# A fused retention and feed-forward block: the order of the first loads and the length of the warming

## The reference

```python
q1, k1 = apply_rotary(x @ Wq, x @ Wk)              # 4 heads of 64
v = x @ Wv                                         # 4 heads of 128
o = chunk_retention(q, k, v, gamma)                # decay gamma^distance, causal
o = rmsnorm(o, gn_weight) * silu(x @ Wg)
x = layernorm(x + o @ Wo)
h = silu(x @ (w_gate/127).T) * (x @ (w_up/127).T)  # hidden 768, integer weights
x = layernorm(x + h @ (w_down/127).T)
```

## Time and profile before

| | us |
|---|---|
| median of 3 runs | 427.47 |
| lowest and highest | 426.11, 428.21 |
| the profiled execution, its own time | 425.66 |
| its span, first to last instruction | 423.9 |

### The profile page before, as it was taken

How to read it: one execution, slowest core, us unless ns; L and a number is a source line. 1 busy time by engine, 2 the same in 40 slices (tenths; PEclk the granted TensorE clock), 3 DMA queues, 4 the chain that set the end, 5 groups by cost and what they waited for, 6 DMA issues and landing times.

```text
span 423.9 us, 12406 instructions
## 1 busy us (share of the span) xinstructions
PE 418.1 (99%) x4311; PEld 396.8 (94%) x4311; DVE 312.1 (74%) x907; ACT 259.0 (61%) x796; POOL 188.1 (44%) x330
## 2 busy tenths in 40 slices
PE   8999999999999999999999999999999999999995
PEld 7899999999999999999999999999999999999995
DVE  4999677678676778766777666777766777667785
ACT  6568755577566566566566566565666565565552
POOL 2522343445544344444354444354534354444465
PEclk9999999999999999999999999999999999999999
DMA  8931010201111011110001111011110010100002
GB/s 275 376 120 52 0 53 1 65 2 39 39 40 39 2 40 39 39 37 17 27 31 37 37 37 37 0 37 37 37 37 12 1 40 15 39 14 2 15 27 65
DMA packets 14327, 19.66 MB, mean 46 GB/s; under 512 B 1488, under 2 KB 9808, under 8 KB 14288
## 3 DMA queue, kind: packets, MB, share of 16 engines
q1 hardware_dynamic: 14144, 19.08, 13.8%
q10 hardware_dynamic: 144, 0.07, 0.1%
HBM read 14.94 MB, written 4.19 MB: 45 GB/s over the span
## 4 chain that ended last, share of the span: by engine, by line
PE 97%; DVE 1%; issue 0%; POOL 0%; ACT 0%; POOLq 0%; ACTq 0%; DVEq 0%
PE b_rows L463 29%; PE b_ffn L463 20%; PE b_rows L481 13%; PE b_rows L477 8%; PE b_head L639 7%; PE b_head L609 4%; PE b_turn L673 3%; PE b_head L605 3%; PE b_ffn L628 3%; PE b_turn L491 2%; PE b_state L658 2%; PE b_state L745 1%; DVE wf_int L1367 1%; PE b_rows L524 0%; PE b_ffn L658 0%
## 5 line engine op out<-in xcount | busy, mean ns | idle before, releaser
L1710 POOL TENSOR_TENSOR h_lo<-wf_int,h_hi 128x256 fp32r<-128x256 f32 x96 | 70.9, 740 | 97.3 <-ACT h_hi L1005 97.0
L463 PE MATMUL b_ffn<-x1T_hi,wf_hi 128*128 128x256 f32 x384 | 92.6, 278 | 0.1
L463 PE MATMUL b_ffn<-x1T_lo,wf_hi 128*128 128x256 f32 x384 | 92.1, 277 | 0.0
L463 PEld LDWEIGHTS b_ffn<-x1T_hi,wf_hi 128*128 128x128 f32 x384 | 72.2, 188 | 0.7 <-DVE wf_int L1344 0.5
L463 PEld LDWEIGHTS b_ffn<-x1T_lo,wf_hi 128*128 128x128 f32 x384 | 72.2, 188 | 0.0
L980 ACT ACTIVATE sq<-b_head 128x128 f32<-128x128 f32 x124 | 34.4, 277 | 50.5 <-PE b_head L639 47.5
L1005 ACT CAST h_hi<-wf_int 128x256 fp32r<-128x256 f32 x96 | 38.8, 404 | 40.6 <-DVE wf_int L1344 39.9
L1728 POOL TENSOR_TENSOR ve<-mv,eps 128x1 f32<-128x1 f32 x63 | 13.7, 217 | 87.3 <-DVE mv L1455 71.0
L481 PE MATMUL b_rows<-wp_hi,xT_lo 128*128 128x256 f32 x198 | 50.0, 277 | 0.0
L1344 DVE TENSOR_TENSOR wf_int<-b_ffn,wf_int 128x256 f32<-128x256 f32 x96 | 40.4, 421 | 11.8 <-ACT wf_int L994 9.0
L1446 DVE TENSOR_TENSOR z<-b_rows,x_sb 128x256 f32<-128x256 f32 x32 | 13.6, 425 | 44.7 <-PE b_rows L463 44.7
(11 more groups left out here) (158 smaller groups left out, 1227.4 us busy)
## 6 DMA issues: line engine op xcount, KB each, us to landing
xT_raw<-in_xT SPq DMA_DIRECT2D x16, 256.0 KB, 2.7
x_sb<-in_x SPq DMA_DIRECT2D x16, 256.0 KB, 2.7
out<-wf_int SPq DMA_DIRECT2D x30, 128.0 KB, 1.7
wf_int<-in_w_ffn SPq DMA_DIRECT2D x6, 384.0 KB, 6.3
wf_int<-in_w_proj SPq DMA_DIRECT2D x6, 256.0 KB, 4.2
rope_sb<-in_rope SPq DMA_DIRECT2D x4, 256.0 KB, 5.7
rope_q<-in_rope_by_row SPq DMA_DIRECT2D x2, 512.0 KB, 8.8
wo_raw<-in_w_o SPq DMA_DIRECT2D x1, 512.0 KB, 6.8
```

The lines of the kernel that those rows point to most:

```text
L463: mm = pe.matmul(dst, a, b, start=(i == 0 and j == 0 and not begun), stop=(i == n - 1 and j == len(passes) - 1 and not more), skip_group_c ...
L1710: pool.tensor_tensor(h_lo[:, ring, hb], h_full[:, u], h_hi[:, ring, hb].bitcast(F32), ALU.subtract).then_inc(h_split[j], 1)
```

## The change

ScalarE issues the load of W(0,0) itself, as its first instruction. SP's first load is now the x of tile 0 alone (128 KB), followed by the five other weight parts, and the x of tile 1 comes behind them, in front of the rope tables. The array of pair 0 is laid out by tile on the host so that each half is one piece of 1 KB in a row; its target in SBUF is two pieces of 512 bytes per partition. ScalarE casts the six weight parts one after the other and tile 1's x behind them. The warming has six products instead of eight. The same bytes are loaded in all.

```diff
-WARM_UP = 8
+WARM_UP = 6
...
+        xT_first_in = sem("xT_first_in")
...
-            def load_w_proj(c):
-                for k in range(KD):
+            def load_w_proj(c, parts=range(KD)):
+                for k in parts:
                     sp.dma_start(wp_raw[:, c, k], w_proj[c, k]).then_inc(wp_in[KD * c + k], 16)
 
-            load_xT(0, 0)
-            load_w_proj(0)
+            def load_xT_of_pair_0(tile):
+                part = xT[0:P, tile * KD * P:(tile + 1) * KD * P].rearrange("p (k n) -> p k n", k=KD)
+                sp.dma_start(xT_raw[:, 0, :, tile * P:(tile + 1) * P], part).then_inc((xT_first_in, xT_in[0])[tile], 16)
+
+            load_xT_of_pair_0(0)
+            load_w_proj(0, (1,))
             load_w_proj(1)
             load_w_proj(2)
+            load_xT_of_pair_0(1)
             sp.dma_start(rope_sb[:, 0], rope[0]).then_inc(rope_in[0], 16)
...
             def split_xT(s, q, t):
 
                 ring, at = t // 2, (t % 2) * P
-                act.wait_ge(xT_in[ring], 16 * (q + 1))
+                if is_slot(s, 0):
+                    act.wait_ge(xT_first_in, 16)
+                else:
+                    act.wait_ge(xT_in[ring], 16 * (q + 1))
...
+            act.dma_start(wp_raw[:, 0, 0], w_proj[0, 0]).then_inc(wp_in[0], 16)
             act.wait_ge(filled, 1)
             act.activation(silu_first[:], half_neg[:, 0:1], ACT.Silu)
...
             split_xT(0, 0, 0)
-            split_w_proj(0, 0)
-            split_xT(1, 0, 1)
-            split_w_proj(0, 1)
-            for c in (1, 2):
+            for c in range(3):
                 for k in range(KD):
                     split_w_proj(c, k)
+            split_xT(1, 0, 1)
...
+    xT = laid(x.reshape(-1, 2 * P, KD, P).transpose(0, 3, 2, 1))
+    xT[0] = laid(xT[0].reshape(P, KD, 2, P).swapaxes(1, 2)).reshape(P, KD, 2 * P)
...
-        "in_xT": laid(x.reshape(-1, 2 * P, KD, P).transpose(0, 3, 2, 1)).reshape(-1, KD * 2 * P),
+        "in_xT": xT.reshape(-1, KD * 2 * P),
```

## The result

| | before | changed |
|---|---|---|
| median of 22 runs each, us | 426.25 | 427.26 |
| lowest, highest, us | 425.23, 428.21 | 426.21, 429.29 |
| the profiled execution, us (span) | 425.66 (423.9) | 429.29 (427.6) |

The ratio of the changed kernel to the one before is 1.0024, 95% interval 1.0013 to 1.0034: about 1 us slower. The median came out where it was forecast (427.3), but only because the 22 runs of before have a lower median, 426.25, than the three that the forecast started from; against them the change cost 1 us where it was to give 0.2. The profiled execution of the changed kernel is its slowest of the 22, which has to be kept in mind when reading its rows.

What follows compares the result with a forecast made beforehand. TensorE, 99% busy, bounds the kernel and carries start changes to the end; its 0.4 to 0.45 us gain shrinks to 0.2 at slot 0's turn, waiting for rotation. Profiled 425.66 becomes 425.46, median 427.47 becomes 427.3; range 425.7 to 428.8 us.

Steps and rivals of the forecast that it cites:

- rival C: ScalarE's start: the table load goes before the W(0,0) issue, slot 1's first nine end 0.25 us later; median 427.7, chance 0.12.
- rival A: Start of slot 1: tile 1's x comes last and holds slot 1, 0.2 us later than before; median 427.7, chance 0.09.
- at half the size it comes at 3.1 to 3.4, I take 3.3: First load on SP: tile 0's x, halved, lands at 3.3 us instead of 3.42; its cast ends at 3.7.
- I take 3.7: W(0,0) from ScalarE's queue lands at 3.7 us instead of 4.06; first product at 4.4, 0.45 earlier, bounds 0.1 and 0.7.
- the hole at 2.2 us: DMA at 2.2 to 2.4 us, 113 GB/s: a second issuing queue may fill it, worth 0 to 0.2 us.
- up at about 7.1 as before: Slot 0 on TensorE: clock rises at about 7.1 us as before, so slot 0 ends at 10.0 instead of 10.47.
- rival B: Slot 0 on TensorE: less warming and a hole delay the clock, 0.2 us per slow product, +1.8; median 429.3, chance 0.09.
- slot 0's first products follow closely, as before: Slot 0's start: the prediction's argument against a later clock rise, which had cost +1.8 us and chance 0.09.
- hardly moves: 9.69, less 0 to 0.2: Rope table 0's load on SP: same bytes ahead, lands 0 to 0.2 us before 9.69; rotation starts at 9.6.
- the 0.2 us of gain: Slot 0's turn: the rotation's earlier start gives 0.2 us, bounds 0.1 and 0.4; the rest of TensorE's gain is waited off.
- S: Start loads, theory after the result: ScalarE's queue shares the DMA engines, so tile 0's x lands late; no chance given.

Runs made afterwards that it cites:

- e2: The kernel before with six warming products instead of eight, nothing else changed; ratio 1.0010 to the kernel before.
- e4: The changed kernel with W(0,0) issued by SP right behind tile 0's x instead of by ScalarE, six warming products; ratio 1.0019 to the kernel before.
- e7: The changed kernel with W(0,0) issued by SP and eight warming products, leaving the split of x and the cast order; ratio 0.9999 to the kernel before.
- e8: As e7, but pair 0's x lands in a buffer of its own in 1 KB pieces instead of 512 bytes; ratio 0.9994 to the kernel before.
- e1: The changed kernel with eight warming products instead of six; ratio 1.0002 to the kernel before.
- e5: The kernel before with no warming products instead of eight; ratio 1.0024 to the kernel before.
- g2: The kernel before with seven warming products instead of eight; ratio 1.0034 to the kernel before.
- f4: The kernel before, unchanged, run again for a second profile only; not timed, slot 0's turn at 12.54 us.
- e6: The kernel before with one edit, ScalarE issuing W(0,0) as its first instruction, eight warming products; ratio 1.0009 to the kernel before.
- f2: The changed kernel with ten warming products instead of six; ratio 0.9989 to the kernel before.
- g1: The kernel before with six warming products begun 1.2 us later, so that no hole is left; ratio 0.9999 to the kernel before.
- f3: The kernel before with ten warming products instead of eight; ratio 1.0009 to the kernel before.

## Why the prediction was wrong

- *What held.* TensorE carries the start's time unchanged to the end (turn 2.23 us later in the chain and 2.09 in the timeline, last activation 2.02; 16 profiles of 16). The issue on ScalarE's queue is early and hidden (rival C fell). Warming ends at 4.00. Two products fewer gave 0.1 us at the front (e2), though the first product of two other profiles on the old loads scatters as much (4.91 and 4.92). Casting tile 1's x last is covered in the changed kernel (11.27 against 12.70), and is not where the time went (rival A fell). The rotation did not bound the changed kernel: it was done at 12.74 (11.98 + 0.76), 1.9 us ahead of the turn.
- *The first step that failed*: "at half the size it comes at 3.1 to 3.4, I take 3.3". It landed at 4.4. W(0,0), "I take 3.7", landed at 0.82 + 3.4 = 4.22, behind the latest time allowed for it, 4.06. I gave ScalarE's queue a price for its own load only and none for the load beside it. The stretches show it (length, engines busy, clock, DMA share, GB/s), the kernel before and then the changed one:

```profile
1.80:2.40 0.60, 0.60 (x5) 0.60 (x4) 0.00 (x0) 0.51 (x2) 0.35 (x2) 1.00 0.89 174
2.40:3.00 0.60, 0.60 (x5) 0.60 (x5) 0.00 (x0) 0.00 (x0) 0.00 (x0) 1.00 0.95 362
```

```profile
1.80:2.40 0.60, 0.60 (x5) 0.60 (x4) 0.00 (x0) 0.60 (x1) 0.35 (x2) 1.00 0.25 69
2.40:3.00 0.60, 0.60 (x5) 0.60 (x5) 0.00 (x0) 0.38 (x2) 0.00 (x0) 1.00 1.04 273
```

and e4, where SP is alone but the pieces are small:

```profile
2.40:3.00 0.60, 0.60 (x5) 0.60 (x5) 0.00 (x0) 0.00 (x0) 0.00 (x0) 1.00 0.98 214
```

From 2.4 to 3.0 us the kernel before moves 362 GB/s, all of it for SP's queue; the changed one moves 273, shared between both. Here is that stretch of the changed kernel by queue (q10 is ScalarE's, q1 SP's): packets, MB, share of the time of the 16 DMA engines.

```profile
q10 hardware_dynamic: 60, 0.12, 81.7%
q1 hardware_dynamic: 80, 0.04, 22.4%
```

W(0,0) moved three times the bytes of x while x was what everything waited for. In the other five profiles with two queues ScalarE's queue took 49 to 61% of the engines in this stretch and SP's 25 to 41%. Nor did the second queue fill the hole at 2.2 us: from 1.8 to 2.4 us the six profiles with two queues moved 41 to 130 GB/s, the ten with one 85 to 280. So the Trainium skill's rule (DMA: Bandwidth & Descriptors, "Issuing engines are not separate DMA queues") was worth more than the upper bound I made of it: as it says, the transfers interleave. What the rows add is that the one that everybody waits for pays as well. The small pieces have a price too (from 2.4 to 3.0 us 214 GB/s in e4 and 260 in e7, 307 with the 1 KB pieces of e8, 277 to 403 in the seven profiles with x whole and one queue), which eats what the smaller load was to give: in e4 W(0,0) landed at 4.04 behind the half, in the kernel before at 4.06 behind the whole. The first product was 0.65 us late where it was to be 0.45 early.
- *The step that cost the time*: the clock "up at about 7.1 as before", and with it the chance of 0.09 for rival B. Rival B named the mechanism, its place (a hole of half a microsecond where there was none) and its price, 0.2 us for each product at the low level. The hole became 1.5 us (4.00 to 5.50), because of the first failure, and nine products more were slow: 1.58 us in that execution. With six products and a hole the fall came at 9.5 to 11.5 us in five profiles of five, turn 13.5 to 14.6, mean 13.8; with eight or ten it came by 7.1 in seven of eight, turn 12.5 to 13.2 (the eighth, e1, 14.2), mean 12.9. The difference of the means, 0.9 us, is about the 1.0 us of the result. What went wrong in the weighing: "slot 0's first products follow closely, as before" was no argument, as one profile with a rise at 7.1 did not show how much of the margin the warming was.
- *The sum's own term.* Rope table 0 that "hardly moves: 9.69, less 0 to 0.2" was what the 0.2 us of gain stood on, and the last weight part was to land near 8.05, at 8.5 at the latest. They landed at 10.38 and near 9.3. More than that: in the seven profiles with the old loads all on SP rope table 0 landed anywhere from 8.8 (e2) to 10.2 (e5), so the term is smaller than its own scatter from one execution to the next. Even with both failures above taken away (e7, e8) nothing of the 0.2 us was measured. The turn is at 12.47 to 12.56 in five profiles with an early clock, whatever the first product's time (4.78 to 5.55), but not for one reason: in the kernel before and in g2 its weight load waited 0.41 and 0.44 us for the rotation, in f4, e6 and e8 it followed slot 1's products. That the loads set this floor is argued, not shown.

What is shown and what is argued: S is shown directly. That the late clock, not S, carries most of the loss rests on e4 against e7 (same loads; six: 1.0019, turn 13.53; eight: 0.9999, turn 12.97) and on f2. The single intervals are wide and overlap, and it is the table as a whole that says it: the five timed sets with six products and a hole have ratios of 1.0010 to 1.0024, the six with eight or ten 0.9989 to 1.0009. g1 (0.9999) and g2 (1.0034) stand outside this order.

The table also says more on hole and amount. In the six profiles in which the clock was still low at the end of the warming and a hole of 0.7 us or more followed, the fall came at 9.5 us or later, with eight products (e1) as with six. Where the clock was low and the hole was at most 0.5 us, it came at 5.6 to 8.5 (the kernel before, e7, f3, g1, g2). Where the clock was up before the warming ended, holes of 0.3 to 1.1 us did no harm (f4, e6, e8, f2); that was so in four of the eight profiles with eight or ten products and in none of the seven with six or seven. So the hole matters where the clock is still low, and more warming may make that rarer; the second half rests on few profiles, and g2's timed runs stay unexplained. No version was measured faster than the kernel before; e7 and e8, level with it, showed no loss.

## What to carry to other kernels

A second issuing queue at the start is not free for the first: if one small load releases everything, let it run alone, and start the others behind it. Let the warming products reach up to the first real product: six profiles of six with a hole of 0.7 us or more behind a warming that ended at the low level had the late clock. So price a cut in them together with whatever moves that product, and assume the slow level for the stretch rather than the rise that one profile happened to show. Where the effect is a microsecond and runs of one kernel differ by three, follow one event of the profile (here slot 0's turn) over several kernels instead of the total.

## What the runs showed of the hardware that was not expected

- The last store of 64 KB took 1.7 to 3.6 us from issue to landing, from one execution to the next of nearly the same program.
- Leaving out all eight warming products (fall at 10.8 us, turn at 14.36) was hardly worse than leaving out two with a hole behind the rest (falls at 9.5 to 11.5, turns at 13.5 to 14.6).
- Once the clock was up, a hole of 0.8 to 1.1 us in front of the first product did not bring the slow level back (f2, e6).
- In the changed kernel two queues with 256 KB and 128 KB issued at the same moment delivered them at 4.2 and 4.4 us, where one queue of the kernel before delivered 256 KB at 3.4 and the next 256 KB at 4.1.
